# Moving seven of 32 multiplications by u from VectorE to GpSimd, with a two-way sum of y, in an AdaLN, Mamba and expert-mixture kernel

## The chip, the cores and the metric

The kernel runs on one core of a Trainium2 chip. The metric is the device time of one execution in microseconds. The kernel before takes 4711.0 us (the median of three runs, 4710.68 to 4715.38).

## What is computed

The input x has 4 sequences of 2048 tokens of width 512. A modulation (six rows of 512 for each sequence) scales and shifts a layer norm ahead of each of two sub-layers and scales the result that is added to x. The second sub-layer is a mixture of 8 experts, two of them chosen for each token, and a shared one. The first is a Mamba layer, and its core is where the change lies. For each of 512 channels and each of 16 states it computes, from Delta, B, C and u of the token:

```python
dA = Delta[..., None] * A
A_bar = jnp.exp(dA)
B_bar = jnp.expm1(dA) / (dA + 1e-06) * Delta[..., None] * B_proj[:, :, None, :]

def step(h, inp):
    a_t, b_t, c_t, u_t = inp
    h = a_t * h + b_t * u_t[..., None]
    y_t = jnp.sum(h * c_t[:, None, :], axis=-1)
    return (h, y_t)
```

## The kernel before

The tokens are cut into 16 blocks of 512 (q), the channels into 4 groups of 128. A **unit** is 128 channels x 1024 columns, so there are 32 units. Most of them are one group of channels over two blocks; the first four and the last four are two groups over one block. A unit has 16 states, so the work of the scan is 512 **states** (c), each a chain of passes over a 128x1024 tile, and a loop over slots, one a state, writes out by hand what each engine does. A window is 32 slots (r is the slot in it), about one block's share of all other work. That other work is in the step functions, which hang projections, layer norms, routing and experts on fixed places of the window. Engines run their instructions in the order written and wait for one another by semaphores.

For state c the passes are these. ScalarE makes `inv` (a square, a logarithm, an exponential, in batches of four states), `th` (a tanh) and `abar` (an exponential), L754 to L776. GpSimd multiplies `inv` by `th` two slots ahead (`weight`, L1387). TensorE spreads row B of the state over the 128 partitions into PSUM (L1158), where the tile X has two buffers. VectorE multiplies X by u (`times_u`, L1175), by abar + 1 (`times_abar`, L1181), by `inv` (`times_weight`, L1187), by a ratio (L1194), and runs the scan into `hs` (L1205). In the next slot GpSimd multiplies `hs` by C in place (`times_C`, L1360 or L1363, in half of the windows after a small copy of the carry, L1356), and then, after its step of the window and the `weight` of state c + 2, issues a transfer that adds `hs` to `ysum` (`add_to_y`, L1374). Each such transfer waits for the one before, since all add to one tile; the first of a unit is a plain copy (L1371), and it waits until the last unit's `ysum` has been multiplied by the gate (`gate_y`, L1380, in slots 1 and 17). `hs` has four buffers: the scan of state c waits until the sum of state c - 4 has landed. GpSimd's other steps are eight multiplications of hidden tiles by expert gates (L1449, in slots 18, 19, 22, 23, 24, 29, 30, 31), a Newton step for 1/Delta (slots 7 to 9 and 25 to 27), the splitting of B into three bfloat16 parts (slots 14 to 16) and a normalisation (slot 10). In the first slots it also scales the expert weights (L1426).

SyncE issues all other transfers in one queue. In each slot it first waits for `times_C` of the slot before it and loads the next row of C (L680); then come the loads of weights and rows that the window has there, among them `load_w1` (L544) and `load_gate_row` (L564). The diagonal matrices `dga`, which add the residual in TensorE, are built from the identity and a column of the modulation once for each sequence: four passes over 128x128 on VectorE (L1293, slot 4), used by TensorE in slot 5.

The lines that set the order around the change:

```python
times_weight(c)
...
times_ratio(c)
times_u(c + 1)
scan(c)
times_abar(c + 1)
```

for VectorE, and for GpSimd:

```python
times_C(c - 1)
...
weight(c + 2)
if r in (1, 17):
    gate_y(c // N - 1)
add_to_y(c - 1)
```

## Time and profile before

| | |
|---|---|
| median of three runs | 4711.0 us |
| the profiled execution, its own time | 4710.88 us |
| its span | 4709.1 us |
| mean granted TensorE clock | 0.885 of full speed |
| TensorE busy | 3847.4 us (82%) |
| VectorE busy | 4045.4 us (86%) |
| ScalarE busy | 3970.8 us (84%) |
| GpSimd busy, issuing of transfers not counted | 3646.5 us (77%) |

The shares are means over the span. The first 230 us are set-up; then come 64 states in units over one block, with little TensorE work; then 384 states in which everything runs together, twelve windows; then the last 64 states; and the last 190 us are TensorE's alone. Busy times of GpSimd are rough: the records of its passes overlap the next one's, so its work is better read from the distance between starts. Idle time of an engine that isn't the bottleneck costs nothing.

### The profile page before, as it was taken

Reading aid. Unit: us, or ns where it says so; the run is one execution under the profiler, and the core shown is the slowest. Engines: PE = TensorE matmul, PEld = TensorE weight load, DVE = VectorE, ACT = ScalarE, POOL = GpSimd, SP = SyncE. Lnnn points to the kernel's source line nnn. Section 1 sums busy time; section 2 is a strip of 40 time slices with the busy share of each in tenths; the row PEclk is TensorE's granted clock in tenths of the full one; section 3 lists DMA queues with packets and bytes.
Section 4 is the critical chain, followed back from the end, with each engine's and each line's share of the span. In section 5 each row is a group of like instructions: output and inputs, shape, how many; then the busy total and the mean of one; then the engine's idle time right before and its main releaser. Section 6 shows DMA issues by size and latency. Waiting matters only on the chain.

```text
span 4709.1 us, 37136 instructions
## 1 busy us (share of the span) xinstructions
PE 3847.4 (82%) x9708; PEld 1616.2 (34%) x9708; DVE 4045.4 (86%) x3896; ACT 3970.8 (84%) x4394; POOL 3646.5 (77%) x2304
## 2 busy tenths in 40 slices
PE   6624514899899988998999998899999977988889
PEld 3201201334333333333343433343333433333444
DVE  1288799999999999999999999999999997888820
ACT  2688898998989998999989898989999897888811
POOL 0399987887889888888889888888889896767721
PEclk7856756999999999999999999999999988989889
DMA  4588867888888888788888888888888876657542
GB/s 130 202 243 263 241 168 204 235 237 252 236 248 236 254 238 259 219 250 255 237 259 231 253 235 245 236 260 231 249 253 235 243 215 168 186 159 200 148 131 67
DMA packets 352221, 1037.19 MB, mean 220 GB/s; under 512 B 41253, under 2 KB 44389, under 8 KB 344710
## 3 DMA queue, kind: packets, MB, share of 16 engines
q1 hardware_dynamic: 278282, 766.35, 47.6%
q0 software_dynamic: 73728, 268.47, 28.7%
q8 instruction: 78, 1.28, 0.1%
q14 instruction: 133, 1.09, 0.1%
HBM read 639.74 MB, written 126.51 MB: 163 GB/s over the span
## 4 chain that ended last, share of the span: by engine, by line
ACT 23%; PE 20%; issue 13%; DVE 12%; DMA 10%; POOL 9%; SPq 0%; POOLq 0%; DVEq 0%; ACTq 0%
PE ps L1121 8%; DMA ysum<-hs 8%; PE ps L1140 5%; ACT inv L761 4%; PE ps L1091 3%; ACT th L772 3%; ACT inv L767 3%; ACT inv L754 3%; ACT abar L776 3%; DVE ps L1187 2%; DVE ps L1181 2%; POOL inv L1387 2%; DVE ps L1175 2%; POOL hs L1360 2%; DMA w1r<-in_W 2%
## 5 line engine op out<-in xcount | busy, mean ns | idle before, releaser
L1387 POOL TENSOR_TENSOR inv<-inv,th 128x1024 f32<-128x1024 f32 x512 | 1270.3, 2481 | 162.2 <-ACT th L772 161.0
L1121 PE MATMUL ps<-hf,w1r 128*128 128x512 f32 x2304 | 1117.0, 638 | 107.9 <-DMA w1r<-in_W 65.3
L1360 POOL TENSOR_TENSOR hs<-hs,Cb 128x1024 f32<-128x1024 f32 x384 | 977.5, 2546 | 39.7 <-DVE hs L1205 23.1
L1140 PE MATMUL ps<-w2r,hid 128*128 128x512 f32 x1776 | 821.5, 610 | 0.4 <-issue 0.3
L1158 PE MATMUL ps<-Brow,pick 48*128 48x512 bf16 x1024 | 343.9, 420 | 574.4 <-DVE hs L1205 573.3
L1175 DVE SCALAR_TENSOR_TENSOR ps<-ps,us 128x1024 f32<-128x1024 f32 x512 | 627.9, 1226 | 174.4 <-PE ps L1158 174.2
L754 ACT ACTIVATE inv<-nrd,kappa 128x1024 f32<-128x1024 f32 (+1 forms) x640 | 577.9, 968 | 181.3 <-DVE ps L1187 177.2
L1374 POOL DMA_DIRECT2D ysum<-hs x480 | 444.7, 926 | 350.9 <-DMA ysum<-hs 344.2
L1121 PEld LDWEIGHTS ps<-hf,w1r 128*128 128x128 f32 x2304 | 456.2, 205 | 689.6 <-issue 634.1
L1194 DVE SCALAR_TENSOR_TENSOR ps<-nrd,inv_kappa,ps 128x1024 f32<-128x1024 f32 (+1 forms) x640 | 675.1, 1073 | 15.6
L1205 DVE TENSOR_TENSOR_SCAN hs<-abar,carry,ps 128x512 f32<-128x512 f32 (+1 forms) x384 | 683.2, 1800 | 0.3
L1187 DVE SCALAR_TENSOR_TENSOR ps<-ps,inv 128x1024 f32<-128x1024 f32 x512 | 627.5, 1226 | 45.6 <-POOL inv L1387 23.2
L776 ACT ACTIVATE abar<-delta,negA 128x1024 f32<-128x1024 f32 (+1 forms) x640 | 605.8, 966 | 61.2 <-DVE hs L1205 61.0
L1181 DVE SCALAR_TENSOR_TENSOR ps<-abar,ps 128x1024 f32<-128x1024 f32 x512 | 617.6, 1206 | 0.1
L767 ACT ACTIVATE inv<-inv,ln_coef 128x1024 f32<-128x1024 f32 (+1 forms) x640 | 607.3, 968 | 1.5
L772 ACT ACTIVATE th<-delta,halfA 128x1024 f32<-128x1024 f32 (+1 forms) x640 | 605.4, 965 | 0.7 <-POOL inv L1387 0.7
L1205 DVE TENSOR_TENSOR_SCAN hs<-abar,ps 128x1024 f32<-128x1024 f32 (+1 forms) x256 | 511.4, 2008 | 0.3
L1140 PEld LDWEIGHTS ps<-w2r,hid 128*128 128x128 f32 x1776 | 336.3, 194 | 456.1 <-issue 455.2
L761 ACT ACTIVATE inv<-inv 128x2048 f32<-128x2048 f32 x256 | 478.9, 1902 | 1.3
L1158 PEld LDWEIGHTS ps<-Brow,pick 48*128 48x128 bf16 x1024 | 58.6, 97 | 932.4 <-DVE hs L1205 698.3
L1363 POOL TENSOR_TENSOR hs<-hs,Cb 128x1024 f32<-128x1024 f32 x128 | 310.5, 2426 | 38.1 <-DVE hs L1205 30.1
L1244 DVE TENSOR_TENSOR x<-ps,x 128x512 f32<-128x512 f32 x256 | 171.6, 681 | 169.7 <-PE ps L1140 150.5
(155 smaller groups left out, 5044.6 us busy)
## 6 DMA issues: line engine op xcount, KB each, us to landing
ysum<-hs POOLq DMA_DIRECT2D x512, 512.0 KB, 5.6
Cb<-c_rows SPq DMA_DIRECT2D x384, 512.0 KB, 4.6
w1r<-in_W SPq DMA_DIRECT2D x144, 512.0 KB, 5.5
w2r<-w_scaled SPq DMA_DIRECT2D x141, 512.0 KB, 7.0
Cb<-c_rows SPq DMA_DIRECT2D x128, 256.0 KB, 3.9
gbc<-expert_gates SPq DMA_DIRECT2D x128, 256.0 KB, 5.2
aw<-in_W_val SPq DMA_DIRECT2D x64, 256.0 KB, 6.1
xa<-in_x SPq DMA_DIRECT2D x32, 512.0 KB, 7.4
```

Of the source, the lines that this page charges most:

```text
L754: ins = s.activation(inv[:, c % 6, cols], nrd[:, u % 2, cols], ACT.Square, bias=1.0, scale=kappa[:, c % N, g:g + 1])
L767: ins = s.activation(inv[:, c % 6, cols], inv[:, c % 6, cols], ACT.Exp, scale=-1.0, bias=ln_coef[:, c % N, g:g + 1])
L772: ins = s.activation(th[:, c % 3, cols], delta[:, u % 2, cols], ACT.Tanh, scale=halfA[:, c % N, g:g + 1])
L776: ins = s.activation(abar[:, c % 4, cols], delta[:, u % 2, cols], ACT.Exp, scale=negA[:, c % N, g:g + 1])
L1121: mm = t.matmul(o, w1r[:, n % 2, k, h * P:(h + 1) * P], hf[:, k, :], start=(k == 0), stop=(k == G - 1))
L1140: mm = t.matmul(o, hidden(e)[:, h, tt * P:(tt + 1) * P], (last_w2(e) if q == NQ - 1 and grp == 1 else w2r[:, e % 3])[:, h, :], start=(grp ...
L1175: v.scalar_tensor_tensor(X(c), X(c), 1.0, us[:, u % 2, :], ALU.mult, ALU.mult).then_inc(uB_done, 1)
L1181: v.scalar_tensor_tensor(X(c), abar[:, c % 4, :], 1.0, X(c), ALU.add, ALU.mult).then_inc(p1_done, 1)
L1187: v.scalar_tensor_tensor(X(c), X(c), 1.0, inv[:, c % 6, :], ALU.mult, ALU.mult).then_inc(pw_done, 1)
L1205: ins = v.tensor_tensor_scan(hs[:, c % 4, cols], abar[:, c % 4, cols], X(c)[:, cols], 0.0 if begins(u) else carry[:, g, c % N:c % N + 1], ...
L1360: gp_.tensor_tensor(hs[:, c % 4, :], hs[:, c % 4, :], Cb[:, c % 2, :], ALU.mult).then_inc(hC_done, 1)
L1387: gp_.tensor_tensor(inv[:, c % 6, :], inv[:, c % 6, :], th[:, c % 3, :], ALU.mult).then_inc(thinv_done, 1)
```

## The change

- In the states 4, 6, 8, 13, 15, 22 and 30 of each window of 32 GpSimd multiplies `inv` by u too, right behind its product of `inv` and `th` (a new pass, L1411 of the changed kernel). VectorE's `times_u` falls away for these states; its `times_abar` then reads the spread B as TensorE left it.
- `ysum` has two halves. Even states are added to one, odd states to the other, each with a semaphore of its own, so a sum waits for the one two states earlier. `gate_y` first adds the halves (a new pass, twice a window), and two states of a unit are plain copies.
- `hs` has three buffers where it had four, and the scan waits for the sum of state c - 3.
- `add_to_y(c - 1)` stands right behind `times_C(c - 1)`, ahead of GpSimd's step and of `weight(c + 2)`; only in slots 1 and 17 it stays behind `gate_y`.
- The diagonal matrices `dga` are made on ScalarE.
- SyncE issues the load of the last expert's W1 in slot 24 ahead of the gate row 6.

```diff
-        hs = sb("hs", [P, 4, TB])
-        ysum = sb("ysum", [P, TB])
+        hs = sb("hs", [P, 3, TB])
+        ysum = sb("ysum", [P, 2, TB])
...
+        U_BY_POOL = (4, 6, 8, 13, 15, 22, 30)
...
+            if r == 24:
+                load_w1(qf, 8)
             if r in (18, 19, 22, 23, 24):
                 load_gate_row(qf, {18: 2, 19: 3, 22: 4, 23: 5, 24: 6}[r])
...
-            if r == 24:
-                load_w1(qf, 8)
...
+            def diagonal(q):
+                if has(q) and q % QPB == 0:
+                    ge(act, mm_out, TPB * q)
+                    for g in range(G):
+                        ins = s.activation(dga[:, g, :], identity[:], ACT.Identity, scale=col(q // QPB, M_GA, g))
+                    ins.then_inc(f_dga, 1)
...
             def times_u(c):
-                if 0 <= c < NC:
+                if 0 <= c < NC and c % WIN not in U_BY_POOL:
...
             def times_abar(c):
                 if 0 <= c < NC:
                     dve.wait_ge(abar_done, c + 1)
-                    dve.wait_ge(uB_done, c + 1)
+                    if c % WIN in U_BY_POOL:
+                        dve.wait_ge(B_ready, c + 1)
+                    else:
+                        dve.wait_ge(uB_done, products_with_u(c))
...
-                    if c >= 4:
-                        dve.wait_ge(y_summed, 16 * (c - 3))
+                    if c >= 3:
+                        dve.wait_ge(y_summed[(c - 3) % 2], 16 * ((c - 3) // 2 + 1))
...
             def add_to_y(c):
                 if 0 <= c < NC:
                     pool.wait_ge(hC_done, c + 1)
-                    if c % N == 0:
+                    if c % N < 2:
                         ge(pool, y_gated, unit(c))
-                        gp_.dma_start(ysum[:], hs[:, c % 4, :]).then_inc(y_summed, 16)
+                        gp_.dma_start(ysum[:, c % 2, :], hs[:, c % 3, :]).then_inc(y_summed[c % 2], 16)
                     else:
-                        pool.wait_ge(y_summed, 16 * c)
-                        gp_.dma_start(ysum[:], hs[:, c % 4, :], accum_op=ALU.add).then_inc(y_summed, 16)
+                        pool.wait_ge(y_summed[c % 2], 16 * (c // 2))
+                        gp_.dma_start(ysum[:, c % 2, :], hs[:, c % 3, :], accum_op=ALU.add).then_inc(y_summed[c % 2], 16)
...
             def gate_y(u):
                 if 0 <= u < NU:
-                    pool.wait_ge(y_summed, 16 * N * (u + 1))
+                    for odd in range(2):
+                        pool.wait_ge(y_summed[odd], 16 * (N // 2) * (u + 1))
+                    gp_.tensor_tensor(ysum[:, 0, :], ysum[:, 0, :], ysum[:, 1, :], ALU.add).then_inc(y_joined, 1)
+                    pool.wait_ge(y_joined, u + 1)
                     pool.wait_ge(gate_ld, 16 * (u + 1))
-                    gp_.tensor_tensor(gy[:], ysum[:], gy[:], ALU.mult).then_inc(y_gated, 1)
+                    gp_.tensor_tensor(gy[:], ysum[:, 0, :], gy[:], ALU.mult).then_inc(y_gated, 1)
...
+                    if c % WIN in U_BY_POOL:
+                        pool.wait_ge(thinv_done, c + 1)
+                        pool.wait_ge(us_ld[u % 2], 16 * (u // 2 + 1))
+                        gp_.tensor_tensor(inv[:, c % 6, :], inv[:, c % 6, :], us[:, u % 2, :], ALU.mult).then_inc(weighted_u, 1)
...
             times_C(c - 1)
+            if r not in (1, 17):
+                add_to_y(c - 1)
...
             weight(c + 2)
             if r in (1, 17):
                 gate_y(c // N - 1)
-            add_to_y(c - 1)
+                add_to_y(c - 1)
```

The first place is GpSimd in slots 19 and 20 of a window in the middle: `carry` and `hs` are `times_C`, `inv` is the weight, `ysum<-hs` the sum. Before:

```order
L1356 COPY carry<-hs 128x1 [waits C_loaded_0,scan_done]
L1360 TENSOR_TENSOR hs<-hs,Cb 128x1024 [waits carry_done]
L1449 TENSOR_TENSOR hid<-hid,gbc 128x1024 [waits gate_rows_loaded_1,gelu_done]
L1387 TENSOR_TENSOR inv<-inv,th 128x1024 [waits tanh_done,inverse_done]
L1374 DMA ysum<-hs 128x1024 [waits y_summed,hC_done]
L1356 COPY carry<-hs 128x1 [waits C_loaded_1,scan_done]
L1360 TENSOR_TENSOR hs<-hs,Cb 128x1024 [waits carry_done]
L1387 TENSOR_TENSOR inv<-inv,th 128x1024 [waits tanh_done,inverse_done]
L1374 DMA ysum<-hs 128x1024 [waits y_summed,hC_done]
```

The same slots in the changed kernel:

```order
L1373 COPY carry<-hs 128x1 [waits C_loaded_0,scan_done]
L1377 TENSOR_TENSOR hs<-hs,Cb 128x1024 [waits carry_done]
L1391 DMA ysum<-hs 128x1024 [waits even_states_summed,hC_done]
L1475 TENSOR_TENSOR hid<-hid,gbc 128x1024 [waits gate_rows_loaded_1,gelu_done]
L1407 TENSOR_TENSOR inv<-inv,th 128x1024 [waits tanh_done,inverse_done]
L1373 COPY carry<-hs 128x1 [waits C_loaded_1,scan_done]
L1377 TENSOR_TENSOR hs<-hs,Cb 128x1024 [waits carry_done]
L1391 DMA ysum<-hs 128x1024 [waits odd_states_summed,hC_done]
L1407 TENSOR_TENSOR inv<-inv,th 128x1024 [waits tanh_done,inverse_done]
L1411 TENSOR_TENSOR inv<-inv,us 128x1024 [waits u_loaded_1,tanh_times_inverse_done]
```

The sum has moved up to stand directly behind the pass whose result it sends, and state 22's weight is followed by the product with u.

The second place is SyncE in slot 24 of the same window: `w1r` is W1 of an expert, `gbc` a gate row. Before:

```order
L680 DMA Cb<-c_rows 128x1024 [waits hC_done]
L688 DMA us<-u_rows 128x1024 [waits uB_done,u_stored]
L697 DMA Brow<-b_parts 48x1024 [waits B_ready,b_stored]
L564 DMA gbc<-expert_gates 128x512 [waits gated_hidden]
L544 DMA w1r<-in_W 128x1024 [waits mm_w1]
```

In the changed kernel:

```order
L690 DMA Cb<-c_rows 128x1024 [waits hC_done]
L699 DMA us<-u_rows 128x1024 [waits weight_times_u,uB_done,u_stored]
L708 DMA Brow<-b_parts 48x1024 [waits B_ready,b_stored]
L554 DMA w1r<-in_W 128x1024 [waits mm_w1]
L574 DMA gbc<-expert_gates 128x512 [waits gated_hidden]
```

The last expert's W1 no longer stands behind the gate row, which waits for GpSimd's fifth gating of the block.

## Rows read from the trace of the kernel before

**Rows 1.** Busy us of each engine in three stretches, clock, DMA share, GB/s.

```profile
core 0: us, PE busy (x) PEld busy (x) DVE busy (x) ACT busy (x) POOL busy (x), PEclk, DMA share, GB/s
230.00:780.00 550.00, 190.43 (x416) 64.87 (x416) 490.67 (x499) 489.51 (x674) 493.55 (x323) 0.61 0.78 225
1000.00:3400.00 2400.00, 2178.91 (x5517) 905.88 (x5517) 2312.17 (x2074) 2219.29 (x2227) 2046.74 (x1269) 0.94 0.85 245
3875.00:4520.00 645.00, 547.24 (x1380) 241.65 (x1381) 507.00 (x575) 495.67 (x672) 454.12 (x283) 0.88 0.63 171
```

**Rows 2.** Groups by line and shape, 1000:3400: busy us, mean ns, idle before.

```profile
L1387 POOL TENSOR_TENSOR inv<-inv,th 128x1024 f32<-128x1024 f32 x297 | 752.3, 2533 | 46.4 <-ACT th L772 46.2
...
L1356 POOL COPY carry<-hs 128x1 f32<-128x1 f32 x132 | 58.9, 446 | 0.0
...
L1293 DVE TENSOR_SCALAR dga<-identity,modc 128x128 f32<-128x128 f32 x8 | 12.1, 1575 | 0.0
```

**Rows 3.** VectorE, who waited for whom, 1000:3400: us, times, longest.

```profile
DVE ps L1175 <- PE ps L1158: 50.8, 30, 5.0
```

**Rows 4.** Timeline of GpSimd: start, length, line, operation, [idle before it].

```profile
2002.26 2.64 POOL L1387 TENSOR_TENSOR inv<-inv,th 128x1024 f32<-128x1024 f32 x1
2004.57 1.17 POOL L1374 DMA_DIRECT2D ysum<-hs  x1
2005.18 2.96 POOL L1360 TENSOR_TENSOR hs<-hs,Cb 128x1024 f32<-128x1024 f32 x1
2007.50 2.95 POOL L1449 TENSOR_TENSOR hid<-hid,gbc 128x1024 f32<-128x1024 f32 x1
```

**Rows 5.** GpSimd, who waited for whom, 1000:3400.

```profile
POOL ysum L1374 <- DMA ysum<-hs: 253.9, 93, 6.2
POOL inv L1387 <- ACT th L772: 46.2, 23, 4.0
```

**Rows 6.** Timeline of VectorE: start, length, line, operation.

```profile
2002.26 1.23 DVE L1175 SCALAR_TENSOR_TENSOR ps<-ps,us 128x1024 f32<-128x1024 f32 x1
2003.39 2.34 DVE L1205 TENSOR_TENSOR_SCAN hs<-abar,carry,ps 128x1024 f32<-128x1024 f32 x1
```

**Rows 7.** TensorE, who waited for whom, 1000:3400.

```profile
PE ps L1121 <- DMA w1r<-in_W: 47.2, 9, 6.8
```

**Rows 8.** The chain of waits, 2004:2020: start, length, what.

```profile
2008.14 2.32 POOL hid L1449
...
2010.84 7.68 DMA w1r<-in_W
```

**Rows 9.** Timeline of GpSimd, a dependent and an independent follower.

```profile
1934.70 0.60 POOL L1458 CAST bc_sb<-bc_sb 16x512 bf16<-16x512 f32 x1
1935.38 1.15 POOL L1461 TENSOR_TENSOR bc_sb<-bc_sb 16x512 f32<-16x512 f32 x1
...
1941.74 0.60 POOL L1458 CAST bc_sb<-bc_sb 16x512 bf16<-16x512 f32 x1
1942.31 2.35 POOL L1387 TENSOR_TENSOR inv<-inv,th 128x1024 f32<-128x1024 f32 x1
```

**Rows 10.** Timeline of GpSimd at the end of a unit.

```profile
1950.97 2.38 POOL L1380 TENSOR_TENSOR gy<-ysum,gy 128x1024 f32<-128x1024 f32 x1
1953.93 0.60 POOL L1371 DMA_DIRECT2D ysum<-hs  x1 [0.58 <-POOL gy L1380]
1954.54 2.37 POOL L1360 TENSOR_TENSOR hs<-hs,Cb 128x1024 f32<-128x1024 f32 x1
```

**Rows 11.** The line L1371: what its engine waited for before it.

```profile
  POOL gy L1380: 20.0, 31
```

**Rows 12.** GpSimd line L1387 alone (one pass a state), first stretch.

```profile
230.00:780.00 550.00, 152.96 (x65) 0.61 0.78 225
```

**Rows 13.** The line L1374 in 1000:3400: landing time of the sum transfers.

```profile
DMA to landing us min/median/max: 4.5/6.1/11.5
```

**Rows 14.** The line L1175 in 1000:3400: durations ns min/median/max.

```profile
L1175 DVE SCALAR_TENSOR_TENSOR ps<-ps,us x296: 1217/1225/1233, 1004.8 to 3393.2; 128x1024 f32<-128x1024 f32 x148
```

More of the change, by code:

```diff
@@ L384, in adaln_mamba_moe @@
         thinv_done, hC_done = sem("tanh_times_inverse_done"), sem("hC_done")
+        weighted_u = sem("weight_times_u")
         B_ready, uB_done, p1_done, pw_done, bu_done, scan_done = (
             sem("B_ready"), sem("uB_done"), sem("abar_plus_1_done"), sem("weighted_done"), sem("bu_done"), sem("scan_done"))
-        y_summed, y_gated, carry_done = sem("y_summed"), sem("y_gated"), sem("carry_done")
+        y_summed = [sem("even_states_summed"), sem("odd_states_summed")]
+        y_joined, y_gated, carry_done = sem("y_joined"), sem("y_gated"), sem("carry_done")
         a_stat, a_log, a_rstd, a_shift, a_xn = (
@@ L451, in adaln_mamba_moe, with products_by_pool, products_with_u @@
         BLOCK_OF = [k for k in range(NK) for u in range(FIRST_U[k], FIRST_U[k + 1])]
+        U_BY_POOL = (4, 6, 8, 13, 15, 22, 30)
+        def products_by_pool(c):
+            return sum(1 for i in range(c + 1) if i % WIN in U_BY_POOL)
+        def products_with_u(c):
+            return c + 1 - products_by_pool(c)
         def starts(u):
@@ L686, in sync_slot @@
                     sp.wait_ge(st_u, 16 * fronts(u))
-                ge(sp, uB_done, N * (u - 1))
+                ge(sp, uB_done, products_with_u(N * (u - 1) - 1))
+                ge(sp, weighted_u, products_by_pool(N * (u - 1) - 1))
                 sp.dma_start(tile_of(us[:, u % 2, :], u), rows_of(u_d, u)).then_inc(us_ld[u % 2], 16)
@@ L898, in act_steps @@
                 if place == "start":
+                    diagonal(qf)
                     silu_of_u(qa)
@@ L1184, in times_weight @@
                 if 0 <= c < NC:
-                    dve.wait_ge(thinv_done, c + 1)
+                    dve.wait_ge(weighted_u if c % WIN in U_BY_POOL else thinv_done, products_by_pool(c) if c % WIN in U_BY_POOL else c + 1)
                     dve.wait_ge(p1_done, c + 1)
@@ L1201, in scan @@
                     dve.wait_ge(bu_done, c + 1)
[L1202 to L1203 removed]
+                    if c >= 3:
+                        dve.wait_ge(y_summed[(c - 3) % 2], 16 * ((c - 3) // 2 + 1))
                     for cols, g in parts(u):
[L1205 removed]
+                        ins = v.tensor_tensor_scan(hs[:, c % 3, cols], abar[:, c % 4, cols], X(c)[:, cols],
                                                    0.0 if begins(u) else carry[:, g, c % N:c % N + 1], ALU.mult, ALU.add)
@@ L1289, in early @@
             def early():
-                if r == 4 and has(qf) and qf % QPB == 0:
-                    ge(dve, mm_out, TPB * qf)
-                    for g in range(G):
-                        ins = v.tensor_scalar(dga[:, g, :], identity[:], col(qf // QPB, M_GA, g), None, ALU.mult)
-                    ins.then_inc(f_dga, 1)
                 if r == 8 and has(qf):
@@ L1356, in times_C @@
                         gp_.tensor_copy(carry[:, g:g + n, c % N:c % N + 1],
-                                        hs[:, c % 4, :].rearrange("p (g t) -> p g t", g=n)[:, :, TB // n - 1:TB // n]).then_inc(carry_done, 1)
+                                        hs[:, c % 3, :].rearrange("p (g t) -> p g t", g=n)[:, :, TB // n - 1:TB // n]).then_inc(carry_done, 1)
                         pool.wait_ge(carry_done, carries(c))
                     if len(parts(u)) == 1:
-                        gp_.tensor_tensor(hs[:, c % 4, :], hs[:, c % 4, :], Cb[:, c % 2, :], ALU.mult).then_inc(hC_done, 1)
+                        gp_.tensor_tensor(hs[:, c % 3, :], hs[:, c % 3, :], Cb[:, c % 2, :], ALU.mult).then_inc(hC_done, 1)
                     else:
-                        both = hs[:, c % 4, :].rearrange("p (g t) -> p g t", g=2)
+                        both = hs[:, c % 3, :].rearrange("p (g t) -> p g t", g=2)
                         gp_.tensor_tensor(both, both, Cb[:, c % 2, 0:T].unsqueeze(1).broadcast_to([P, 2, T]),
```

1 line of the change is left out of this document (removed).

## The prediction

> **What bounds the kernel now.** I read four views in this order: busy time by stretch, then the idle time of each engine and what ended it, then the timeline of GpSimd by the distance between starts, then the chain of waits at one recurring stall.
>
> In the steady stretch VectorE is busy 2312.2 of 2400 us, 96.3%, ScalarE 92.5%, TensorE 90.8% [rows 1]. It holds 297 states [rows 2], so a state takes 8.08 us and a window of 32 states 258.6 us. The reader is to see there that VectorE is the bound, and by how little: ScalarE's 2219.3 us are 239.1 us a window. VectorE's largest idle item, 50.8 us, is `times_u` waiting for the spread B [rows 3].
>
> GpSimd looks free at 85% [rows 1], but that column leaves out the issuing of transfers, and the distance between starts tells more. `weight` to the sum's issue is 2.31 us, the issue to the next pass 0.61, `times_C` to the next pass 2.32 [rows 4]. So a state costs GpSimd 2.32 + 2.31 + 0.61 = 5.24 us, or 167.7 a window. Eight gatings add 18.6, 14.2 carry copies (132 in 297 states) of some 0.54 us 7.7 [rows 2], two `gate_y` with the issue behind them about 6, the Newton passes about 11: 211 us, and the normalisation and the split of B some 8 more, 219. From above: 2400 less its two large waits, 253.9 for the sum before and 46.2 for ScalarE [rows 5], is 2099.9 us, 226.2 a window, small waits included. I take 221.5. GpSimd is thus truly occupied 86% of a window, and idle mostly because sums queue behind one another.
>
> **The change, part by part**, for a window of 32 states.
>
> Product with u taken off VectorE: from the start of `times_u` to that of the scan is 1.13 us [rows 6]. Seven times: -7.9 us. `dga`: eight passes take 12.1 us in 2400 [rows 2], -1.3 us a window; on ScalarE it is bounded by nothing and by twice that, and hidden, since ScalarE has 19 us to spare.
>
> W1 ahead of the gate row: once a window TensorE waits about 5 us for the last expert's W1 (47.2 us in nine) [rows 7]. The chain shows why: a gating on GpSimd of 2.3 us, then SyncE, then a transfer of 7.7 us [rows 8]. The load no longer waits for that gating, so it lands up to 2.9 us earlier; most of the 50.8 us of VectorE's waits stand around this stall. Gain if VectorE is the bound: up to 2.9 us; if GpSimd is, nothing. The gate row now stands behind W1's wait, which ended before; its gating is four slots later.
>
> VectorE would so need 258.6 - 7.9 - 1.3 - 2.9 = 246.5 us a window. That is the floor from its side, and with ScalarE at 239 it could nearly be reached.
>
> Two-way sum: the 253.9 us of waits for the sum before go, 27 us a window of GpSimd. They cost time now only where GpSimd is late, and they are already outside my 221.5. A join is a two-input pass more for each unit, 2 x 2.42 = 4.8 us.
>
> Product with u put on GpSimd: a pass of 2.31 us directly behind the one it depends on. What dependence costs between two passes is seen at the split of B: the dependent pass starts after 0.68 us, an independent one after 0.57 [rows 9]. So 7 x 2.42 = 16.9 us.
>
> The **moved issue** is the term that decides. Today the sum's issue stands behind `weight`, and the pass it depends on has long ended, so it follows after 2.31 us. In the change it depends on the pass just ahead. There is one such place in the kernel: the plain copy behind `gate_y` starts 2.96 us after that pass [rows 10], with 20.0 us of idle time in 31 cases, 0.65 us each [rows 11], and the next pass still comes 0.61 us after it. Thirty of 32 sums come into that position (slots 1 and 17 are there already): 30 x 0.65 = 19.5 us. The nearest rows for a bound below are the dependent passes, 0.1 us, so 3 us; above, I take 0.8 us, 24 us, to allow for a wait that is now ahead of the transfer's own. I take 0.65, since it is the same kind of issue on the same engine.
>
> The Trainium skill (DMA: Bandwidth & Descriptors, "Anatomy of one DMA — SWDGE (gpsimd) path") puts sequencer dispatch at about 50 ns. By that the gap would be nearer the 0.1 us, which is the first rival below.
>
> GpSimd: 221.5 + 16.9 + 4.8 + 19.5 = **262.7 us a window, more than the 258.6 that a window takes now.** GpSimd becomes the bound, 16 us above VectorE's floor, and the gains on VectorE are spare. I add no stalls, because both other engines have over 10 us of slack a window. Steady part: +4.1 x 12 = +49 us.
>
> First 64 states: 550 us with GpSimd busy 493.6, VectorE 490.7 [rows 1]; 65 passes of `weight` there [rows 12]. Of its 56 free us some 18 are issues (about 0.28 us of each isn't covered by a record), 38 are idle. Added: 60 x 0.65 + 14 x 2.42 + 4 x 2.42 = 39 + 34 + 10 = 83 us. If all idle time could be used it is +45, less what the removed waits let flow: +40. Last 64 states: GpSimd 454 of 645 us [rows 1], so its 83 us fit; W1 earlier, -5.
>
> **Sum:** 49 + 40 - 5 = +84 us on the profiled execution's 4710.9, 4795. The median of the runs is 4711.0, the same.
>
> **The rivals.**
>
> *One: the issue waits no longer than a pass does.* For it: dependent passes cost 0.1 us [rows 9]. Against it: 31 cases of 0.65. GpSimd then needs 262.7 - 30 x 0.55 = 246.2, beside VectorE's 246.5. Three engines near 97% don't reach their floors; with 2.5 us of stalls a window is 249, -9.6 x 12 = -115; in the first 64 states 50 us of work meet 38 idle and the relief of VectorE, +5; last ones -5. **4596**, say 4600. It is faster. It decides below a gap of about 0.5 us, where GpSimd's sum falls under 258.6.
>
> *Two: the third `hs` buffer.* Three states are 24.2 us. Off them go the scan, 2.34 [rows 6], `times_C` up to the issue, 2.96, and the landing, 6.1 at the median and 11.5 at most [rows 13]. That leaves GpSimd 12.8 and 7.4 us to be late. Sums now overlap, on transfer engines busy 85% [rows 1], so landings near 11.5 us may be usual; then the scan waits for the sum and GpSimd for the scan. At 5 us a window on top of my sum, 14 windows: +70, **4865**. Against it: a GpSimd that is the bound can be idle only after its lateness is used up.
>
> *Three: the shared port.* Today `times_u` takes 1217 to 1233 ns whatever GpSimd does [rows 14], which speaks against any mutual blocking. If VectorE stood still for the seven new passes it would need 246.5 + 16.2 = 262.7 too, and two engines at one bound would stall each other some 3 us: +3 x 12, **4830**. The Trainium skill (Perfetto Trace Analysis, "Optimizing Scalar/DVE Operations") warns that GpSimd and VectorE share an SBUF read port, so that moving work between them might not help. By that rule, with this trace against it, the change would be this third case.
>
> **How the numbers follow.** GpSimd as the bound, my forecast: 0.60, of which 0.53 slower, 0.05 within 0.2%, 0.02 faster, since its own range is 4730 to 4860 (GpSimd's occupation 219 to 226). Rival one: 0.25, of which 0.02 within 0.2%. Rival two: 0.12, slower. Rival three: 0.03, slower. About 0.2% (9 us) is what a measurement of this kernel can tell from no change. So faster 0.25, same 0.07, slower 0.68. Cases of both signs hold much of the chance, so the range takes in rival one's time and rival two's: 4600 to 4865; the likeliest case alone is 4730 to 4860.
>
> **What would show it.** In the trace after: GpSimd's sum issues start about 2.96 us after `times_C`, with idle time put down to that pass, some 0.6 us each; the waits for the sum before nearly gone; starts of the new pass about 2.4 us behind `weight`; VectorE's `times_weight` waiting for GpSimd by 10 to 15 us a window, VectorE busy about 92%; TensorE's wait for W1 down from 5 us to 2 to 3; scan waits for a sum near nothing. Wrong if the issue follows `times_C` after 2.4 us, or if GpSimd shows idle time for other reasons while the window is over 262 us: then the buffers or ScalarE's batches bind it. A window near 250 us with VectorE at 96% would be rival one.

## The result, and the profile after

The changed kernel takes 4762.0 us (median of four runs, 4754.9 to 4766.7) against 4710.8 us for the kernel before (four runs, 4708.8 to 4715.4) on the same chip. The ratio is 1.0101, with a 95% interval of 1.0086 to 1.0116: **slower by 1.0%**, in the forecast direction, 33 us under the forecast time. Its profiled execution took 4761.2 us, with a span of 4759.4 us and a mean granted clock of 0.877.

The engines in the page of the changed kernel (busy us, share of the span, instructions):

```profile
PE 3857.9 (81%) x9708; PEld 1622.6 (34%) x9708; DVE 3926.0 (82%) x3768; ACT 3977.9 (84%) x4410; POOL 3994.5 (84%) x2448
```

VectorE has lost 119 us of work and GpSimd has gained 348. The same three stretches as in [rows 1], by windows (columns as there):

```profile
230.00:780.00 550.00, 174.40 (x378) 58.97 (x378) 454.94 (x462) 466.31 (x649) 509.13 (x326) 0.60 0.74 214
1000.00:3400.00 2400.00, 2167.89 (x5480) 905.73 (x5479) 2216.78 (x1978) 2206.33 (x2218) 2232.36 (x1343) 0.93 0.84 242
3875.00:4520.00 645.00, 533.06 (x1356) 234.05 (x1355) 503.68 (x563) 526.48 (x712) 510.82 (x313) 0.87 0.62 172
```

The stretch from 1000 to 3400 us now holds 295 states, so a window of 32 takes 260.3 us where it took 258.6. VectorE's share fell from 96.3 to 92.4%, a window costs it 240.5 us after 249.1. TensorE and ScalarE are a little less busy than before. Only GpSimd's row rose, and in the first stretch it stands at 509 of 550 us, again with a part of its issuing left out. Its waits for other engines and for transfers fell there from 47.7 us to 13.8, of which one row is nearly all (230:780; us, times, longest):

```profile
POOL carry L1373 <- DVE hs L1227: 13.0, 4, 6.8
```

To see where the 50 us of span came from, I cut each trace at the starts of the weight pass (L1387, now L1407) of states 0, 64, 448 and 511. The first and the last piece of each span are taken together as set-up and tail.

| us | states 0 to 64 | 64 to 448 (a window) | 448 to 511 | set-up and tail | span |
|---|---|---|---|---|---|
| before | 552.2 | 3110.3 (259.2) | 608.3 | 438.3 | 4709.1 |
| after | 581.4 | 3130.8 (260.9) | 618.2 | 429.0 | 4759.4 |
| difference | +29.2 | +20.5 (+1.7) | +9.9 | -9.3 | +50.3 |

What GpSimd waited for in the steady stretch (1000:3400; total us, times, longest):

```profile
POOL ysum L1391 <- POOL hs L1377: 84.0, 256, 0.9
POOL inv L1407 <- ACT th L783: 24.2, 24, 2.3
POOL ysum L1397 <- DMA ysum<-hs: 12.6, 11, 1.9
POOL ysum L1388 <- POOL gy L1400: 10.6, 18, 0.9
POOL hs L1377 <- DVE hs L1227: 7.8, 6, 2.2
POOL ysum L1388 <- POOL hs L1377: 5.8, 17, 0.5
POOL carry L1373 <- DVE hs L1227: 0.9, 2, 0.6
```

The waits for a preceding sum [rows 5], 253.9 us, are gone. In their place the sum's issue L1391 stands idle behind the pass `times_C` just ahead of it, 256 times, by 0.33 us each. Waits for anything that GpSimd doesn't make itself add up to 46.4 us (24.2 + 12.6 + 7.8 + 0.9, and 0.9 in two small rows), 5.0 us a window. So GpSimd is occupied by its own work for 260.3 - 5.0 = **255.3 us a window, 98%**, where [rows 5] gave 226.2 at most and the same count over all its waits gives 224.0. It is the engine nearest to its limit. Whether it is what makes a window longer, the experiments have to say.

The timeline of GpSimd shows a moved issue (start, length, line, operation, idle time before it):

```profile
2022.36 2.37 POOL L1377 TENSOR_TENSOR hs<-hs,Cb 128x1024 f32<-128x1024 f32 x1
2025.02 0.88 POOL L1391 DMA_DIRECT2D ysum<-hs  x1 [0.30 <-POOL hs L1377]
2025.63 2.67 POOL L1475 TENSOR_TENSOR xn<-xn,gbc 128x1024 f32<-128x1024 f32 x1
```

The issue starts 2.66 us after `times_C`, and the next pass comes 0.61 us later, as in [rows 4]. Over all 258 cases the distance from `times_C` to the issue has a median of 2.67 and a mean of 2.78 us, since it is about 2.9 us in the 78 cases in which the record of `times_C` itself is over 2.5 us long. An independent follower starts after 2.33 us. By these distances the move costs 0.45 us a sum, not 0.65. The runs with and without it, further down, make it 0.38.

The new pass with u, L1411, in another piece of the same view:

```profile
1156.24 2.66 POOL L1407 TENSOR_TENSOR inv<-inv,th 128x1024 f32<-128x1024 f32 x1
1158.97 2.35 POOL L1411 TENSOR_TENSOR inv<-inv,us 128x1024 f32<-128x1024 f32 x1
1161.29 2.37 POOL L1377 TENSOR_TENSOR hs<-hs,Cb 128x1024 f32<-128x1024 f32 x1
```

It starts 2.73 us after the weight pass it depends on (the median of the 64 cases; the mean is 2.70), and the pass behind it follows after 2.32 us. Groups by line and shape of the stretch, in the columns of [rows 2]:

```profile
L1407 POOL TENSOR_TENSOR inv<-inv,th 128x1024 f32<-128x1024 f32 x295 | 759.9, 2576 | 24.6 <-ACT th L783 24.2
...
L1391 POOL DMA_DIRECT2D ysum<-hs x258 | 228.2, 884 | 84.6 <-POOL hs L1377 84.0 <-ACT th L783 0.6
...
L1411 POOL TENSOR_TENSOR inv<-inv,us 128x1024 f32<-128x1024 f32 x64 | 151.3, 2363 | 5.0
```

VectorE's waits in the stretch:

```profile
DVE ps L1194 <- PE ps L1177: 83.1, 43, 5.1
DVE x L1266 <- PE ps L1113: 41.3, 9, 5.5
DVE ps L1209 <- POOL inv L1407: 25.8, 29, 1.7
DVE hs L1227 <- DMA ysum<-hs: 4.5, 13, 0.7
```

It now waits for GpSimd's weights 25.8 us, 2.8 a window, where it waited 12.5 before, and its wait for the spread B (L1194, formerly L1175) grew from 50.8 us [rows 3] to 83.1. Its pass with u takes what it took [rows 14]:

```profile
L1194 DVE SCALAR_TENSOR_TENSOR ps<-ps,us x230: 1223/1226/1233, 1009.2 to 3396.8; 128x1024 f32<-128x1024 f32 x115
```

TensorE's wait for the last expert's W1 did not shrink. The view of its waits, and the chain at one of these stalls (columns as in [rows 7] and [rows 8]):

```profile
PE ps L1140 <- DMA w1r<-in_W: 70.7, 10, 8.2
...
PE ps L1110 <- issue: 44.7, 9, 6.0
```

```profile
2292.31 2.31 POOL hs L1377
...
2294.64 0.32 SPq L690
...
2295.55 0.38 SPq L708
...
2295.99 10.25 DMA w1r<-in_W
```

W1's load is now ahead of the gate row, but it stands behind the slot's row of C, which waits for `times_C` to end at 2294.63, and behind two more loads. Then it takes 10.25 us to land, where [rows 8] had 7.68. The sums themselves land later too, 8.2 us at the median where it was 6.1 [rows 13]:

```profile
DMA to landing us min/median/max: 6.1/8.2/11.9
```

This goes with the early issue. In the two kernels below that have the halves and the late issue the median of the same line is 6.0 and 6.7 us, and with the early issue and no product it is 8.5.

### The profile page after: what moved, and what is told of

Read it like the earlier page. It is cut to its first block, busy times and chain, and to the rows that moved or that the text cites. A ratio compares the mean times of both kernels' runs of the same rounds, so it can differ in the third digit from the quotient of the medians.

```text
span 4759.4 us, 37221 instructions
## 1 busy us (share of the span) xinstructions
PE 3857.9 (81%) x9708; PEld 1622.6 (34%) x9708; DVE 3926.0 (82%) x3768; ACT 3977.9 (84%) x4410; POOL 3994.5 (84%) x2448
## 4 chain that ended last, share of the span: by engine, by line
PE 24%; ACT 20%; POOL 18%; issue 13%; DVE 12%; DMA 4%; SPq 0%; POOLq 0%; DVEq 0%; ACTq 0%
PE ps L1140 8%; PE ps L1159 7%; POOL inv L1407 5%; POOL hs L1377 5%; PE ps L1110 4%; ACT inv L772 3%; DVE ps L1209 3%; DVE ps L1203 3%; ACT th L783 3%; ACT inv L765 2%; ACT abar L787 2%; ACT inv L778 2%; DVE hs L1227 2%; DVE ps L1194 2%; DMA ysum<-hs 2%
## 5 line engine op out<-in xcount | busy, mean ns | idle before, releaser
L1407 POOL TENSOR_TENSOR inv<-inv,th 128x1024 f32<-128x1024 f32 x512 | 1316.4, 2571 | 85.1 <-ACT th L783 84.4
L1377 POOL TENSOR_TENSOR hs<-hs,Cb 128x1024 f32<-128x1024 f32 x384 | 933.9, 2432 | 23.7 <-DVE hs L1227 8.1
L1209 DVE SCALAR_TENSOR_TENSOR ps<-ps,inv 128x1024 f32<-128x1024 f32 x512 | 627.7, 1226 | 70.3 <-POOL inv L1407 41.6
L1194 DVE SCALAR_TENSOR_TENSOR ps<-ps,us 128x1024 f32<-128x1024 f32 x400 | 491.0, 1227 | 200.1 <-PE ps L1177 199.8
L1203 DVE SCALAR_TENSOR_TENSOR ps<-abar,ps 128x1024 f32<-128x1024 f32 x512 | 617.9, 1207 | 11.9 <-PE ps L1177 11.8
L1391 POOL DMA_DIRECT2D ysum<-hs x448 | 395.8, 883 | 146.7 <-POOL hs L1377 108.9
L1380 POOL TENSOR_TENSOR hs<-hs,Cb 128x1024 f32<-128x1024 f32 x128 | 306.3, 2393 | 31.9 <-DVE hs L1227 24.2
## 6 DMA issues: line engine op xcount, KB each, us to landing
Cb<-c_rows SPq DMA_DIRECT2D x128, 256.0 KB, 3.8
gbc<-expert_gates SPq DMA_DIRECT2D x128, 256.0 KB, 4.7
aw<-in_W_val SPq DMA_DIRECT2D x64, 256.0 KB, 9.1
```

The source lines that it names most:

```text
L1203: v.scalar_tensor_tensor(X(c), abar[:, c % 4, :], 1.0, X(c), ALU.add, ALU.mult).then_inc(p1_done, 1)
L1209: v.scalar_tensor_tensor(X(c), X(c), 1.0, inv[:, c % 6, :], ALU.mult, ALU.mult).then_inc(pw_done, 1)
L1377: gp_.tensor_tensor(hs[:, c % 3, :], hs[:, c % 3, :], Cb[:, c % 2, :], ALU.mult).then_inc(hC_done, 1)
L1407: gp_.tensor_tensor(inv[:, c % 6, :], inv[:, c % 6, :], th[:, c % 3, :], ALU.mult).then_inc(thinv_done, 1)
```

## The experiments

Each kernel ran in rounds beside the kernel before. The middle stretch is given by window as in the table above. Every ratio is to the kernel before as it ran beside, with a median of 4713.5, 4714.4 or 4712.5 us. **Occupied** is the time of GpSimd between two such starts less its waits for other engines and for transfers; it is 224.2 us a window before, and 256.0 after.

**The issue put back behind the step and the weight**, everything else as in the change:

```diff
             times_C(c - 1)
-            if r not in (1, 17):
-                add_to_y(c - 1)
...
             if r in (1, 17):
                 gate_y(c // N - 1)
-                add_to_y(c - 1)
+            add_to_y(c - 1)
```

> The changed kernel with the sum issued behind the weight again in every slot (two halves of ysum, three hs buffers, the product on GpSimd all kept). Theory A (GpSimd is the bound, and the issue behind its own pass costs it about 0.35 us a state, 10.5 us a window): the idle time in front of the issue goes, a window falls from 260.3 us to about 250, total 4620 to 4680. Theory B (the third hs buffer binds): the sums land later, the scan waits for them, 4760 or more. Theory C (TensorE's two stalls a window, W1 of the last expert and the output projection, set the time): within 10 us of 4762.

4729.9 us, ratio 1.0038 (1.0026 to 1.0051). The first 64 states take 563.5 us, 17.9 less than in the change: 60 issues at 0.30 us. A window takes 259.3 us, 1.6 less. GpSimd is occupied 244.6 us of it, 11.4 less than in the change, or 0.38 us an issue. Theory A had the window at 250 us and the time at 4680 at most, so it failed here, and the time lies outside the other two ranges as well. The waits of three engines say more. First VectorE's, then GpSimd's, then TensorE's for W1:

```profile
DVE hs L1227 <- DMA ysum<-hs: 77.8, 36, 5.3
```

```profile
POOL inv L1407 <- ACT th L783: 85.8, 39, 4.6
```

```profile
PE ps L1140 <- DMA w1r<-in_W: 16.8, 9, 3.8
```

With the issue late the third buffer binds: the scan waits for a sum by 77.8 us, where it was 4.5 in the change. GpSimd's relief turns into waiting for ScalarE. So the early issue costs gaps on GpSimd but is what makes three buffers bearable. What a relieved GpSimd would be worth by itself can't be read from this run.

**The product taken away**, everything else as in the change:

```diff
-        U_BY_POOL = (4, 6, 8, 13, 15, 22, 30)
+        U_BY_POOL = ()
```

> The changed kernel with no state's product with u on GpSimd (the set is empty, VectorE makes all 32). Theory A: GpSimd is relieved by 7 x 2.4 = 17 us a window and is at about 238 us, VectorE has 7.9 us more, about 249 busy, and is the bound again: about 256 a window, total 4680 to 4720. Theory B: unchanged, 4750 to 4770. Theory C: within 10 us of 4762.

4747.7 us, 1.0077 (1.0055 to 1.0100). The first 64 states fall by 20.3 us, but a window stays at 261.0. Theory A, with 256 us a window and 4720 at most, failed here too, and none of the three ranges holds the time. Busy times of the stretch, GpSimd's waits, and TensorE's for W1:

```profile
1000.00:3400.00 2400.00, 2165.29 (x5479) 898.51 (x5477) 2281.73 (x2046) 2204.75 (x2217) 2080.61 (x1277) 0.93 0.85 242
```

```profile
POOL inv L1407 <- ACT th L783: 98.5, 40, 4.5
POOL ysum L1391 <- POOL hs L1377: 83.0, 253, 0.9
POOL hs L1377 <- DVE hs L1227: 51.1, 25, 5.2
```

```profile
PE ps L1140 <- DMA w1r<-in_W: 46.7, 9, 8.1
```

GpSimd is occupied 239.1 us a window, 16.9 less, and spends it waiting for ScalarE and the scan. The gaps behind `times_C` stay at 0.33 us. VectorE is back at 95.1% and a window is no shorter, so another bound stands at the same height. What it is in this kernel the rows don't settle.

**Both taken away**: the issue late and no product, so that the two halves, three buffers, `dga` and W1 remain:

```diff
-        U_BY_POOL = (4, 6, 8, 13, 15, 22, 30)
+        U_BY_POOL = ()
...
-            if r not in (1, 17):
-                add_to_y(c - 1)
...
-                add_to_y(c - 1)
+            add_to_y(c - 1)
```

> The changed kernel with no product on GpSimd and the sum issued behind the weight in every slot: two halves of ysum, three hs buffers, the diagonals on ScalarE and W1's order are what is left of the change. Without product but with the early issue a middle window took 261.0 us. If the early issue is what costs there, the window is 259 us and the total 4705 to 4720. If the two halves or the third buffer cost, it stays at 261 and the total at 4735 to 4750.

4743.5 us, 1.0057 (1.0039 to 1.0075). This is what the second of the two expectations said. The first 64 states take 550.9 us, as before the change (552.2): there the halves and the third buffer cost nothing. The early issue alone adds 10.2 us to them, the product alone 12.6, the two together 30.5: the second load finds less idle time left. In the middle it is the other way round. A window takes 262.2 us, 3.0 more than before, although this kernel has neither new load on GpSimd, which is occupied 227.6 us of it. (The profiled execution is the slowest of its eight, 8.2 us over their median; with all of that taken off the middle a window is still 261.5.) Part of it is the third buffer:

```profile
DVE hs L1227 <- DMA ysum<-hs: 34.4, 16, 4.1
```

This run weighs most for the reading of the change. The kernel is 31 us slower than the one before (4743.5 against 4712.5), without the product and without the early issue, and its middle windows are no shorter than those of the changed kernel (260.9). So the two additions to GpSimd are not shown to cost anything in the middle; they are shown to cost 30.5 us in the first 64 states.

**The product alone**, put on the kernel before (its one `ysum`, its four buffers, its late issue):

```diff
+        U_BY_POOL = (4, 6, 8, 13, 15, 22, 30)
...
-                if 0 <= c < NC:
+                if 0 <= c < NC and c % WIN not in U_BY_POOL:
...
+                    if c % WIN in U_BY_POOL:
+                        pool.wait_ge(thinv_done, c + 1)
+                        pool.wait_ge(us_ld[u % 2], 16 * (u // 2 + 1))
+                        gp_.tensor_tensor(inv[:, c % 6, :], inv[:, c % 6, :], us[:, u % 2, :], ALU.mult).then_inc(weighted_u, 1)
```

> The kernel before with the product with u on GpSimd in the seven states and nothing else. Theory A: GpSimd at about 238 us a window without its waits for sums, VectorE at 242, so faster than before, 4650 to 4700, unless the single chain of sums (6.1 us landing, one at a time) makes GpSimd late. Rival: the serial sums, each waited for on GpSimd, leave no room for the seven passes, and it is 4711 or slower.

4721.3 us, 1.0017 (0.9998 to 1.0037), so the rival held and theory A failed. A window takes 259.5 us, 0.3 more than before; the first 64 states 12.9 us more. GpSimd's new work went into time in which it had waited for sums, 253.9 us before:

```profile
POOL ysum L1387 <- DMA ysum<-hs: 94.8, 58, 3.3
POOL inv L1400 <- ACT th L782: 51.1, 23, 4.8
```

```profile
PE ps L1131 <- DMA w1r<-in_W: 68.8, 9, 8.7
```

VectorE's busy time fell by 6.7 us a window (249.3 to 242.6 between the starts), and the window didn't. The relief is idle time now: three other engines are at 91% or more. TensorE's wait for W1, 47.2 us before [rows 7], is 68.8 here, with the sums and SyncE's order as they were.

**W1 alone**, the one move in SyncE's queue put on the kernel before:

```diff
+            if r == 24:
+                load_w1(qf, 8)
             if r in (18, 19, 22, 23, 24):
...
-            if r == 24:
-                load_w1(qf, 8)
```

> The kernel before with the load of the last expert's W1 ahead of gate row 6 and nothing else. If the load is late because of the gating ahead of it, TensorE's wait falls from 5.2 us a window to about 2.5 and the time by up to 2.9 x 14 = 40 us, 4670 to 4700. Rival: the wait is set by something else in SyncE's queue (it was 7.1 us a window in the changed kernel), and the time stays within 10 us of 4711.

4704.4 us, 0.9975 (0.9963 to 0.9988), in the rival's range and short of the 4700 expected at most, with the wait for W1 down from 47.2 to 37.3 us and VectorE's for B from 50.8 to 43.5. There, with VectorE busy 96.6%, the move is worth 9 us.

**W2 behind W1**, in the changed kernel, since three W2 loads of slot 23 stand ahead of W1 in the queue:

```diff
             if r == 24:
                 load_w1(qf, 8)
...
+            if r == 24:
+                load_w2(qf, 2 if qf == NQ - 1 else 1)
...
-            if r == 23:
-                load_w2(qf, 2 if qf == NQ - 1 else 1)
```

> The changed kernel with the three W2 loads of slot 23 (1.5 MB) issued in slot 24 behind the last expert's W1, which they delayed to a landing of 10.25 us. Theory C (TensorE's stalls set the window): TensorE's wait of 7.1 us for W1 falls below 3 us, its following matmuls run at the higher clock, and the time falls by 3 to 5 us a window, total 4700 to 4725. Theory A (GpSimd is the bound, and its passes are unchanged): the wait goes but the time stays within 10 us of 4762.

4766.0 us, 1.0096 (1.0076 to 1.0116). TensorE's wait for W1 fell from 70.7 to 58.5 us only, and the time stayed. Both theories had the wait nearly gone, so this run doesn't test the changed kernel without its stall. The kernels with the late issue come nearer: they wait 16.8 and 22.4 us for W1, and their windows still take 259.3 and 262.2 us.

**ScalarE lighter** and **TensorE lighter**, in the changed kernel. Each leaves out a part of its engine's work:

```diff
-                        s.activation(hidden(e), hidden(e), ACT.Gelu).then_inc(gelu_done, 1)
+                        s.activation(hidden(e)[:, :, 0:8], hidden(e)[:, :, 0:8], ACT.Gelu).then_inc(gelu_done, 1)
```

```diff
-                    for k in range(G):
+                    for k in range(G - h):
...
-start=(k == 0), stop=(k == G - 1))
+start=(k == 0), stop=(k == G - h - 1))
```

> The changed kernel with ScalarE's Gelu applied to 8 of the 512 columns of each half of the hidden tiles only (the rest is left out), about 9 us a window less on ScalarE, nothing else touched. If ScalarE, busy 92%, is the bound of a window with all its waits: 252 us a window, total 4650. If GpSimd is: within 10 us of 4762. Theory D: 2 to 4 us a window, about 4725.

> The changed kernel with one of the four products over channels left out in the second half of each expert's W1 (9 of 72 a window), about 8 us a window less on TensorE. If TensorE with its waits is the bound: 253 us a window, total 4660. If GpSimd is: within 10 us of 4762. Theory D: about 4730.

4752.0 us (1.0068, 1.0050 to 1.0085) and 4744.0 us (1.0049, 1.0030 to 1.0068). The first is just inside what a full GpSimd would give, the second between that and theory D. ScalarE's busy time fell by 7.0 us a window (239.5 to 232.5) and the window by 0.9; TensorE's by 7.2 (234.0 to 226.8) and the window by 0.7. In the second, another 7 us came off the tail, which is TensorE's alone.

**Fourteen products in place of seven**, in the changed kernel:

```diff
-        U_BY_POOL = (4, 6, 8, 13, 15, 22, 30)
+        U_BY_POOL = (2, 4, 5, 6, 8, 12, 13, 15, 19, 22, 23, 28, 30, 31)
```

> The changed kernel with the product with u on GpSimd in fourteen states of 32 in place of seven. Theory A (GpSimd is the bound of the changed kernel everywhere but in the last 64 states): seven passes more are 17 us a window, 278 us a window in the middle and 34 us more in the first 64 states, total about 4990 to 5020, although VectorE has 7.9 us a window less to do. Theory D (the engines share the bound): less than half of that, 4800 to 4870.

4946.8 us (two runs), 1.0490 (1.0458 to 1.0523), between the ranges of theories A and D. A window takes 272.8 us, 11.9 more, and the first 64 states 25.5 us more. Busy times, and VectorE's waits:

```profile
1000.00:3400.00 2400.00, 2089.00 (x5246) 872.05 (x5247) 2068.55 (x1841) 2112.71 (x2120) 2277.95 (x1354) 0.92 0.81 231
```

```profile
DVE ps L1209 <- POOL inv L1411: 72.1, 66, 2.2
DVE hs L1227 <- DMA ysum<-hs: 67.5, 58, 4.6
DVE ps L1209 <- POOL inv L1407: 60.6, 66, 2.4
```

VectorE is down to 86%, and a window is longer. From 1000 to 3400 us GpSimd now waits for nothing but its own passes, so the window of this stretch, 272.3 us, is its own sum: the 255.3 of the changed kernel and 17.0 for seven passes of 2.43 us. Of the 17.0 us the first 5.0 went into the waits that were left, and the rest was paid in full. So the changed kernel stands 5 us short of the point where GpSimd alone sets the window, and anything put on top is paid. That is not the same as GpSimd having made the window longer: taking 17 us from it gave back nothing, taking 11 gave 1.6, and taking 7 us from ScalarE or TensorE gave less than one. In each of these runs something else was in the way, in the first two work or waits that the edit itself brought back to VectorE.

**The early issue alone**, on the kernel before, with its one chain of sums:

```diff
             times_C(c - 1)
+            if r not in (1, 17):
+                add_to_y(c - 1)
...
-            add_to_y(c - 1)
+                add_to_y(c - 1)
```

> The kernel before with the sum issued right behind times_C (but in slots 1 and 17) and nothing else: one ysum, four hs buffers, no product on GpSimd. If the early issue costs by GpSimd's time alone (0.35 us a state), GpSimd's spare 27 us a window take it in the middle and only the first 64 states show it: 15 to 20 us there, total about 4730. If it costs by something else (the sum starts together with the load of the row of C), the middle windows grow as well, by 2 us each, total 4745 to 4755.

4981.7 us, 1.0562 (1.0536 to 1.0588); 279.3 us a window. Both expectations, 4755 at most, were far off. GpSimd's largest wait, and VectorE's:

```profile
POOL ysum L1374 <- DMA ysum<-hs: 427.1, 147, 7.4
```

```profile
DVE ps L1187 <- POOL inv L1387: 129.7, 67, 4.8
```

The wait for the preceding sum grew from 253.9 us [rows 5] to 427.1. It used to fall behind the weight, and now it stands ahead of it, so every late landing delays the weight that VectorE needs. So the early issue needs the two halves of `ysum`.

**The product with the old sums**: the kernel before with the product, `dga` on ScalarE, and W1 ahead of the gate row and of W2, but its one `ysum`, four buffers and late issue. Its difference to the product alone:

```diff
-                if r == 4 and has(qf) and qf % QPB == 0:
-                    ge(dve, mm_out, TPB * qf)
-                    for g in range(G):
-                        ins = v.tensor_scalar(dga[:, g, :], identity[:], col(qf // QPB, M_GA, g), None, ALU.mult)
-                    ins.then_inc(f_dga, 1)
...
+            def diagonal(q):
...
+            if r == 24:
+                load_w1(qf, 8)
             if r in (18, 19, 22, 23, 24):
...
+            if r == 24:
+                load_w2(qf, 2 if qf == NQ - 1 else 1)
```

> The kernel before with the product in seven states on GpSimd, the diagonals on ScalarE, W1 ahead of the gate row and W2 behind W1, and with the sums as they were (one ysum, four hs buffers, issue behind the weight). Theory C: without TensorE's stall VectorE's relief can show, a window of 253 to 256 us, total 4640 to 4680. Theory A (GpSimd too full): no better than 4711, as with the product alone (4721). Theory D (all engines wait for one another round a window, so relief of one only moves the idle time): 4690 to 4710.

4702.6 us, 0.9968 (0.9953 to 0.9983). This is theory D's range. A window takes 257.8 us, but the first 64 states still take 565.0. There, as I read it, the product meets a GpSimd that has the expert weights to scale (L1426, 103.5 us of these states in the kernel before). So the last kernel makes it only for states 64 to 447:

```diff
+        def by_pool(c):
+            return c % WIN in U_BY_POOL and 2 * WIN <= c < NC - 2 * WIN
```

> The kernel with the old sums, the product in seven states, the diagonals on ScalarE, W1 ahead of the gate row and W2 behind W1 (4702.6), with the product only in the states 64 to 447, where GpSimd isn't also scaling the expert weights. If the first 64 and the last 64 states give back the 13 and 6 us that the product cost there, while a middle window stays at 257.8: 4683 to 4693, faster than both kernels. If not, 4700.

**4686.9 us, 0.9939 (0.9920 to 0.9959): faster than both kernels**, by some 25 and 75 us, and in the range expected. The first 64 states are back at 553.6 us, a window takes 257.5. Its busy times, and GpSimd's waits, show that no engine is full:

```profile
1000.00:3400.00 2400.00, 2206.06 (x5573) 921.66 (x5572) 2255.43 (x2017) 2237.08 (x2248) 2217.99 (x1348) 0.94 0.86 247
```

```profile
POOL ysum L1393 <- DMA ysum<-hs: 109.6, 72, 3.8
POOL inv L1406 <- ACT th L785: 30.2, 17, 4.6
```

## Why the prediction was right, and by how much its terms were off

**The mechanism** held in part. GpSimd is filled to 98% of a window, waits for sums are gone, and seven more passes are paid but for 5 us. In the first 64 states the two additions to GpSimd are what costs, 30.5 us. In the middle the step that the forecast rests on did not happen: GpSimd's sum was to pass the 258.6 us that a window took, with 262.7, and it came to 255.3. The prediction put the line between slower and faster at a gap of about 0.5 us. The measured gap, 0.33 us of idle time and 0.45 at most from start to start, lies on the first rival's side of it, and the kernel was slower all the same. The window didn't go down towards VectorE's floor of 246.5 us, and what is left of the change without the two additions costs 3.0 us a window by itself. The sum had nothing for either; the second rival had 5 us a window for the third buffer, on top of a full GpSimd.

**Luck in the total.** The middle was forecast with +49 us and measured with +20.5, the first 64 states with +40 and +29.2, the last with -5 and +9.9, set-up and tail with 0 and -9.3. The direction came out, but the 20 us of the middle are not shown to be GpSimd's.

**GpSimd's sum** was 262.7 us a window and is 255.3, and 5.0 us of waits stand on top of it, where I had added none. Here are its terms, measured in two ways: by distances between starts, with the base as what remains, and by the occupied time of the kernels that have a term and lack it.

| us a window | predicted | by distances | by runs |
|---|---|---|---|
| base | 221.5 | 218.2 (what remains) | 224.2 (before) |
| product with u, 7 x | 2.42 = 16.9 | 2.70 = 18.9 | 2.43 = 17.0 |
| joins | 4.8 | 4.8 | 3.4 |
| moved issues, 30 x | 0.65 = 19.5 | 0.45 = 13.4 | 0.38 = 11.4 |
| waits for others | 0 | 5.0 | 4.9 |
| window | 262.7 | 260.3 | 260.9 |

The last column needs no remainder: 224.2 before, 227.6 with halves and late issue, 244.6 with the product too, 256.0 in the change. The distances overstate both additions, by 4 us together, and why they do is open.

**The moved issue** is the term that was mis-sized. I took the 0.65 us of idle time from [rows 11] as the nearest row, since it is the same kind of issue on the same engine. Behind `times_C` the idle time is 0.33 us, and an issue costs 0.38 by the runs. One row of one situation carried the choice. The Trainium skill's 50 ns of sequencer dispatch (DMA: Bandwidth & Descriptors, "Anatomy of one DMA — SWDGE (gpsimd) path") can't be compared with this directly, since no run here separates the dispatch from the rest of the idle time. Taken alone, as a price for the 0.33 us, it would have been too low by a factor of six to seven.

**The product** starts 2.70 us behind its weight, 0.4 us later than an independent pass would, where I had taken 0.1 us of dependence from small passes [rows 9]. Yet what it adds to GpSimd's occupied time is 2.43 us each (16.9 and 17.0 us a window, with the early issue and with the late one), which is the price forecast.

**Slack of 16 us on VectorE's side.** I wrote that the gains on VectorE are spare, and they were: VectorE lost 8.6 us a window (predicted 9.2) and the window grew. But I had expected VectorE to wait for GpSimd's weights by 10 to 15 us a window, and it was 2.8. Most of VectorE's waiting is for the spread B, 83.1 us. It goes with the early issue: without the product it is 71.6 us, with the issue late 46.2 and 56.0. As I read it, GpSimd's lateness reaches VectorE by the row of C and the W1 load, which SyncE issues behind `times_C`, and by TensorE; no run takes this chain apart.

**W1** went wrong outright. I predicted a wait down from 5 to 2 or 3 us, free of the gating. It rose to 7.1 us each. Alone on the kernel before the move does what I said of it, if less (47.2 to 37.3 us). With W1 moved, the wait is 22.4 us in all with neither addition, 16.8 with the product, 46.7 with the early issue and 70.7 with both. So it is the early issue that brings it back, and the product on top of it. With W1 in its old place the product alone takes it from 47.2 to 68.8. In this slot GpSimd's pass releases the row of C and the sum at the same moment, and W1's load comes behind both; that this is why it lands 2.6 us later is my reading of the chain. I had counted what W1 no longer waits for, and not what now goes out just ahead of it, nor that SyncE reaches it later when `times_C` ends later.

**First 64 states**: predicted +40, measured +29. The runs split it into 10 for the issue alone, 13 for the product alone, and 8 for their meeting. GpSimd is occupied 546 us of these states, 59 more than before, not 83, and its waits fell from 65 to 35 us. So half of the new work found idle time. I had put the idle time of the 550 us stretch at 38 us, and its waits there were 47.7.

**Last 64 states**: predicted -5, measured +10. I had read GpSimd's 454 of 645 us [rows 1] as room for everything. On the kernel before the product alone costs 3.8 us there, and the two halves and three buffers without it 5.5. The last kernel, which has neither, takes 1.6 us more than before. GpSimd still waits 107 us of the changed kernel's 618.2, so it is not full there, and what costs the 9.9 us is open. The tail gave 7 us back, and I tested nothing on it.

**The rivals.** The first, a free issue, was priced by VectorE's floor of 246.5 us plus 2.5. The runs refute the floor. Where the product is made and GpSimd isn't full (the product alone, the version above, the last kernel), a window takes 257.5 to 259.5 us with VectorE at 94%. The kernels nearest to a change without the gap take 4686.9 to 4729.9 us, and from them I estimate some 4700, not 4600. So my range was too wide on that side. The second, the third buffer, isn't in the changed kernel (4.5 us), but it is real as soon as the issue is late (77.8 and 34.4 us) or GpSimd is overfull (67.5 us with fourteen products). The third, a shared port, is refuted here: VectorE's pass with u takes 1226 ns beside seven more GpSimd passes, 1225 before, and the pass by `inv` 1223 in both. The Trainium skill (Perfetto Trace Analysis, "Optimizing Scalar/DVE Operations") names a two-port VectorE operation as the one that locks the port, and says only that moving work between the two might not help. The trace shows no such lock for these passes, which read one operand from PSUM.

**Left open**: what holds a window at 257 to 262 us when GpSimd isn't full. VectorE, ScalarE and TensorE then stand between 90 and 95%, and what one part of the change takes from one engine's waits comes up in another's. Open too is how the 3.0 us a window that the change costs without its two additions divide between the halves and the third buffer: two halves with four `hs` buffers weren't tried.

## What to carry to other kernels

Count an engine that also issues transfers by the distance between the starts of its instructions, not by its busy column, and do it for every stretch: here GpSimd was 87% occupied in the middle and 91% from 230 to 780 us, and the best kernel is the one that adds the work only where there was room. A transfer issued directly behind the pass that it depends on costs the engine a gap each time; it buys an earlier landing, which is worth it only if something waits for the landing. With three engines above 90%, taking some 7 us a window from the fullest gave back two at most, and adding 32 to the one that looked free filled it to 98%. And before an addition is blamed for a longer window, run the kernel without it that keeps all the rest: here that kernel's windows were as long.

## What the runs showed of the hardware

**The gap before a dependent issue isn't the same everywhere.** The plain copies (L1388) wait for `times_C` and for the gating of the unit before. Where the record of the gating comes last the idle time is 0.59 us each, where that of `times_C` comes last 0.34. From the line's own view (us, times):

```profile
  POOL gy L1400: 10.6, 18
  POOL hs L1377: 5.8, 17
```

It is the same instruction and the same semaphores. Whether the order of its two waits makes the difference, or the pass ahead, I did not test.

**TensorE pays for a long wait twice.** After the idle time of 7.43 us before the last expert's W1, 16 matmuls took 9.0 us at a granted clock of 0.76, a mean of two levels: 0.50, that is 1.2 GHz, up to 2309 us, and 1.00, that is 2.4 GHz, from 2311 us on. Just before the wait 17 matmuls took 7.0 us at the full 2.4 GHz. By windows, TensorE alone (busy us, clock, DMA share, GB/s):

```profile
2285.90:2292.90 7.00, 7.00 (x17) 1.00 0.78 171
2306.40:2315.40 9.00, 9.00 (x16) 0.76 0.76 184
```
